# Decoder on one core: tags carried behind the scattered rows, and the last pair's routing in portions of 3 and 1 tiles

## What is computed

```python
xf = x.reshape(N, C)                                   # 2048 tokens, the cross attention's normalised result
topv, topi = jax.lax.top_k(xf @ Wr + br, 2)            # two of 8 experts a token
gates = jax.nn.softmax(topv, axis=-1)
sel = one_hot(topi, E).sum(1)
rank = jnp.cumsum(sel, axis=0) - sel                   # place of the token in its expert's list
keep = (sel > 0) & (rank < cap)                        # cap = 512 places an expert
buf[e, rank] = token                                   # tokens by expert and place
h = gelu(xpad[buf] @ W1 + b1); out = h @ W2 + b2
final[token] += out * gate                             # for each place of each expert
```

## Time and profile before

| | |
|---|---|
| runs | 2364.72, 2367.3, 2368.29 us; median 2367.3 |
| profiled execution | 2387.01 us |
| its span | 2384.8 us |
| PE busy | 2072.3 us, 87% of the span |
| DVE busy | 1717.6 us, 72% |
| ACT busy | 1045.8 us, 44% |
| POOL busy | 334.0 us, 14% |
| mean granted clock of PE | 0.933 |

### The profile page before, as it was taken

How to read it: one execution, slowest core, us unless ns; L and a number is a source line. 1 busy time by engine, 2 the same in 40 slices (tenths; PEclk the granted TensorE clock), 3 DMA queues, 4 the chain that set the end, 5 groups by cost and what they waited for, 6 DMA issues and landing times.

```text
span 2384.8 us, 33574 instructions
## 1 busy us (share of the span) xinstructions
PE 2072.3 (87%) x12364; PEld 1260.1 (53%) x12364; DVE 1717.6 (72%) x2514; ACT 1045.8 (44%) x1641; POOL 334.0 (14%) x368
## 2 busy tenths in 40 slices
PE   6999999999999999885768887988788889839998
PEld 4666666666666666551323344444354445516665
DVE  6677777777777778869999899989998995210001
ACT  1223333322322222237765867587758872202221
POOL 1111111111111111100000000000000001362222
PEclk8999999999999999997789987989899999969999
DMA  6000000000000100011110111011101113112442
GB/s 242 2 0 19 28 26 1 18 28 26 1 18 10 50 2 1 1 38 47 49 60 19 44 52 42 19 36 60 35 19 43 53 36 116 49 26 62 125 124 49
DMA packets 62238, 99.80 MB, mean 42 GB/s; under 512 B 13332, under 2 KB 44591, under 8 KB 61584
## 3 DMA queue, kind: packets, MB, share of 16 engines
q1 hardware_dynamic: 55120, 90.10, 11.6%
q0 software_dynamic: 6976, 7.84, 1.7%
HBM read 83.53 MB, written 15.53 MB: 42 GB/s over the span
## 4 chain that ended last, share of the span: by engine, by line
PE 53%; DVE 28%; issue 10%; ACT 4%; DMA 2%; another core or an unknown queue 1%; POOL 0%; DVEq 0%; SPq 0%; ACTq 0%; POOLq 0%
PE po L1810 9%; PE pa L1800 9%; DVE arena L1561 8%; PE pa L1758 4%; PE po L2378 4%; DVE arena L1551 4%; PE pt L1775 3%; PE pa L2084 3%; PE pa L2367 3%; DVE arena L1158 2%; DVE arena L1569 2%; DMA arena<-rows_to_experts 2%; PE pa L1790 1%; DVE arena L1160 1%; PE pt L1783 1%
## 5 line engine op out<-in xcount | busy, mean ns | idle before, releaser
L2084 PE MATMUL pa<-arena 128*128 128x512 f32 x512 | 297.9, 711 | 85.8 <-DVE arena L1569 85.8
L1561 DVE TENSOR_TENSOR_SCAN arena<-arena 128x1024 f32<-128x1024 f32 x128 | 292.5, 2285 | 13.5 <-ACT arena L937 13.3
L580 POOL TENSOR_SCALAR arena<-arena 128x2 f32<-128x2 f32 (+1 forms) x92 | 27.4, 298 | 1528.2 <-DVE arena L1426 824.7
L1810 PE MATMUL po<-arena 128*128 128x256 f32 x960 | 224.2, 385 | 0.0
L2084 PEld LDWEIGHTS pa<-arena 128*128 128x128 f32 x512 | 100.8, 216 | 218.8 <-DVE arena L1569 117.4
L1800 PE MATMUL pa<-arena 128*128 128x512 f32 x480 | 212.5, 595 | 4.4 <-ACT arena L754 4.1
L776 ACT COPY arena<-pa 128x512 f32<-128x512 f32 x128 | 65.7, 600 | 324.1 <-PE pa L1758 324.1
L1233 DVE TENSOR_TENSOR arena<-pa,arena 128x512 f32<-128x512 f32 x256 | 158.7, 682 | 63.1 <-PE pa L1758 63.0
L921 ACT ACTIVATE arena<-arena 128x510 f32<-128x510 f32 x256 | 170.7, 718 | 55.1 <-DVE arena L1561 51.8
L1810 PEld LDWEIGHTS po<-arena 128*128 128x128 f32 x960 | 176.8, 189 | 32.9 <-issue 6.0
L1701 DVE TENSOR_TENSOR arena<-po,arena 128x512 f32<-128x512 f32 x14 | 9.7, 692 | 231.2 <-PE po L2378 231.2
(11 more groups left out here) (268 smaller groups left out, 3706.6 us busy)
## 6 DMA issues: line engine op xcount, KB each, us to landing
arena<-bc_rows SPq DMA_DIRECT2D x64, 512.0 KB, 4.2
arena<-in_L_ffn_W SPq DMA_DIRECT2D x16, 1024.0 KB, 8.7
arena<-in_L_attn_W SPq DMA_DIRECT2D x8, 1024.0 KB, 5.5
rows_to_experts<-arena SPq DMA_DIRECT2D x4, 1024.0 KB, 13.0
arena<-rows_to_experts SPq DMA_DIRECT2D x8, 512.0 KB
out<-arena SPq DMA_DIRECT2D x5, 512.0 KB, 8.7
arena<-in_x SPq DMA_DIRECT2D x4, 512.0 KB, 7.0
arena<-in_rows SPq DMA_DIRECT2D x8, 256.0 KB, 3.2
```

Source lines behind the costliest of these rows:

```text
L1561: v.tensor_tensor_scan(h.rearrange(flat), decay.rearrange(flat), h.rearrange(flat), 0.0, ALU.mult, ALU.add).then_inc(scan_done, 1)
L1810: last = mm(po[s][:, ts(i, D)], gT[:, c, ts(tile, P)], w2[:, c, :], start=c == 0, stop=c == FM - 1)
L2084: last = mm(pa[c][:, :], ident, uh[i % len(uh)][:, n, :], start=g == 0 and n == 0, stop=g == NS // NG - 1 and n == NG - 1)
```

## The change

**Tags ride behind the rows.** The tile `hst` that holds the rows to be scattered becomes a view of a wider tile `tagged`, 260 numbers a row: the 256 features, then the token's number, its two gates, and the first place of its best expert. A row scatter sends all 260, so `rows_to_experts` has rows of 1040 bytes, and the 32 tag scatters, their DRAM buffer and the tag loads are gone. DVE copies the token numbers into the tile in `weighed`, and per expert finds in `slots_of` which of the two gates belongs to this expert (is the first place of the token's best expert that of this expert or not). The expert part of DVE's program is written out instead of looped, since this comparison needs the expert's number as a constant. `send_rows` now also waits for `tags_ready`.

**The fill.** The zeros go to the first 256 numbers of each row, runs of 1024 bytes instead of 8192; the filling tags go to the last four, 4096 runs of 16 bytes. ACT and POOL wait for both.

**Three portions.** The first 12 tiles are routed as before. The last pair's tiles 12 to 14 get bias, statistics and scaling while the last tile's attention is still under way, and are routed, placed and scattered (6 scatters) as a second portion; tile 15 follows as a third (2 scatters). PE, ACT, DVE and POOL get programs of their own for this. In the first portion, `send_rows` waits for at most 13 of the last pair's 16 value products where it waited for up to 16.

```diff
+TAG = 4
+LAST_TILE = NT - 1
+LAST_THREE = NT - TT
...
-    hst = keep(NT, D)
+    tagged_at = keep.at
+    tagged = keep(NT, D + TAG)
+    hst = tagged[:, :, 0:D]
...
-    lt, rk, base, over = ([a(NT) for _ in range(2)] for _ in range(4))
-    tags = [a(NT, 2) for _ in range(2)]
-    gate = [one[:, :, 1] for one in tags]
+    lt, rk, over = ([a(NT) for _ in range(2)] for _ in range(3))
+    tokens = a(NT)
+    token, gate, base = tagged[:, :, D], [tagged[:, :, D + 1 + k] for k in range(2)], [tagged[:, :, D + 3], a(NT)]
...
-    slot_tags, slot_rows = [a(TT, 2) for _ in range(2)], [a(TT).bitcast(I32) for _ in range(2)]
+    slot_rows = [a(TT).bitcast(I32) for _ in range(2)]
+    slot_gate, slot_part = [a(TT) for _ in range(2)], a(TT)
...
-    xg, xgT, gTe, ye = [a(TT, D) for _ in range(2)], a(KC, W), a(EF // P, W), [a(TT, D) for _ in range(2)]
+    xg, xgT, gTe, ye = [a(TT, D + TAG) for _ in range(2)], a(KC, W), a(EF // P, W), [a(TT, D) for _ in range(2)]
...
-    rows_to = nc.dram_tensor("rows_to_experts", (NE * CAP, D), F32, kind="Internal").ap()
+    rows_to = nc.dram_tensor("rows_to_experts", (NE * CAP, D + TAG), F32, kind="Internal").ap()
-    tags_to = nc.dram_tensor("tags_to_experts", (NE * CAP, 2), F32, kind="Internal").ap()
...
         for q in range(4):
-            sp.dma_start(rows_to.rearrange("(q p r) d -> q p (r d)", q=4, p=P)[q], zero).then_inc(zeroed, 16)
-        sp.dma_start(tags_to, t["tags"]).then_inc(tags_set, 16)
+            sp.dma_start(rows_to.rearrange("(q p r) d -> q p r d", q=4, p=P)[q][:, :, 0:D], zero.rearrange("p (r d) -> p r d", d=D)).then_inc(zeroed, 16)
+        sp.dma_start(rows_to[:, D:D + TAG], t["tags"]).then_inc(zeroed, 16)
...
-            sp.wait_ge(xr_ready, p + 1)
+            sp.wait_ge(xr_ready, p + 1 if p < PAIRS - 1 else PAIRS + 1)
         sp.wait_ge(scattered, 16 * 2 * NT)
         for j in range(2):
             expert_rows(j, j)
-        sp.wait_ge(tags_sent, 16 * 2 * NT)
-        for j in range(2):
-            slot_tags_in(j, j)
...
         def send_rows(first, end, places):
-            pool.wait_ge(zeroed, 16 * 4)
+            pool.wait_ge(zeroed, 16 * 5)
             pool.wait_ge(places_ready, places)
-            pool.wait_ge(xf_kept, end // TT + 1)
+            pool.wait_ge(tags_ready, places)
+            if places == 1:
+                pool.wait_ge(xf_kept, PAIRS)
+            else:
+                pool.wait_ge(xr_ready, PAIRS + places - 2)
             for i in range(first, end):
                 if places == 1:
-                    pool.wait_ge(av2_done, 16 * (PAIRS - 1) + i + 5)
+                    pool.wait_ge(av2_done, 16 * (PAIRS - 1) + min(i + 5, 13))
                 for k in range(2):
                     nc.gpsimd.indirect_dma_start(
-                        out=rows_to, out_offset=bass.IndirectOffsetOnAxis(ap=into[k][:, i:i + 1], axis=0), in_=hst[:, i, :], in_offset=None,
+                        out=rows_to, out_offset=bass.IndirectOffsetOnAxis(ap=into[k][:, i:i + 1], axis=0), in_=tagged[:, i, :], in_offset=None,
                         bounds_check=NE * CAP - 1, oob_is_err=False).then_inc(scattered, 16)
...
             if p is None and n is None:
-                send_rows(0, NT - TT, 1)
+                send_rows(0, LAST_THREE, 1)
+                deviations(GROUPS + groups + 1, 0, TT - 1)
+                deviations(GROUPS + groups + 2, TT - 1, 1)
+                send_rows(LAST_THREE, LAST_TILE, 2)
+                send_rows(LAST_TILE, NT, 3)
+                return
...
-        send_rows(NT - TT, NT, 2)
-        for i in range(NT):
-            for k in range(2):
-                nc.gpsimd.indirect_dma_start(
-                    out=tags_to, out_offset=bass.IndirectOffsetOnAxis(ap=into[k][:, i:i + 1], axis=0), in_=tags[k][:, i, :], in_offset=None,
-                    bounds_check=NE * CAP - 1, oob_is_err=False).then_inc(tags_sent, 16)
...
-                    act.wait_ge(zeroed, 16 * 4)
+                    act.wait_ge(zeroed, 16 * 5)
...
+            def last_rows_out(done, bank, tile, count):
+                act.wait_ge(last_turned, done)
+                nc.scalar.copy(xrT[:, :, tile * P:(tile + count) * P], bank.rearrange("p (k t) -> p k t", k=KC)).then_inc(last_copied, 1)
...
-                        top_gates(0, NT - TT, 1)
+                        top_gates(0, LAST_THREE, 1)
+                    if i == 35:
+                        last_rows_out(1, po[1][:, :], 0, 2)
+                        last_rows_out(2, pt[1][:, 0:S], 2, 1)
+                top_gates(LAST_THREE, LAST_TILE, 2)
+                last_rows_out(3, po[1][:, 0:S], 3, 1)
+                top_gates(LAST_TILE, NT, 3)
...
+            v.tensor_scalar(token[:, at], tokens[:, at], 0.0, None, ALU.add)
...
+            def last_statistics(first, end):
+                rows = xst[:, q * TT + first:q * TT + end, :]
+                dve.wait_ge(wo2_out, 4 * q + end)
+                step.after(v.tensor_tensor(rows, rows, wide(r_xo, end - first), ALU.add))
+                for i in range(first, end):
+                    last = v.bn_stats(out=stats[:, i, :], in_=xst[:, q * TT + i, :])
+                step.apart(last)
+                for i in range(first, end):
+                    last = v.bn_aggr(out=mv[:, i, :], in_=stats[:, i, :])
+                last.then_inc(var_ready, 1)
+            def last_scaled(k, first, end):
+                dve.wait_ge(rstd_ready, cross_group + k)
+                for i in range(first, end):
+                    last = v.tensor_scalar(xr[:, i, :], xst[:, q * TT + i, :], mv[:, i, 0:1], rstd[:, i:i + 1], ALU.subtract, ALU.mult)
+                last.then_inc(xr_ready, 1)
...
+                    if i == 30:
+                        last_statistics(0, TT - 1)
+                    if i == 31:
+                        last_scaled(1, 0, TT - 1)
...
+            if at.lone:
+                last_logits(q + 1, pt[1], LAST_THREE, LAST_TILE)
+                dve.wait_ge(logits_ready, q + 1)
+                compared(LAST_THREE, LAST_TILE)
+                counted(LAST_THREE, LAST_TILE)
+                chosen(LAST_THREE, LAST_TILE)
+                cross(UNITS + 3 + drain)
+                last_statistics(TT - 1, TT)
+                weighed(LAST_THREE, LAST_TILE, 2)
+                ranked(LAST_THREE, LAST_TILE, 2)
+                placed(LAST_THREE, LAST_TILE)
+                last_scaled(2, TT - 1, TT)
+                last_logits(q + 2, pt[0], LAST_TILE, NT)
+                dve.wait_ge(logits_ready, q + 2)
+                compared(LAST_TILE, NT)
+                counted(LAST_TILE, NT)
+                chosen(LAST_TILE, NT)
+                weighed(LAST_TILE, NT, 3)
+                ranked(LAST_TILE, NT, 3)
+                placed(LAST_TILE, NT)
+                return
...
+        def slots_of(e):
+            j = e % 2
+            dve.wait_ge(xg_in[j], 16 * (e // 2) + 16)
+            first, second, best = xg[j][:, :, D + 1], xg[j][:, :, D + 2], xg[j][:, :, D + 3]
+            v.tensor_scalar(slot_rows[j], xg[j][:, :, D], 0.0, None, ALU.add).then_inc(slot_rows_ready, 1)
+            v.scalar_tensor_tensor(slot_part, best, float(CAP * e), first, ALU.is_equal, ALU.mult)
+            step.after(v.scalar_tensor_tensor(slot_gate[j], best, float(CAP * e), second, ALU.not_equal, ALU.mult))
+            step.after(v.tensor_tensor(slot_gate[j], slot_gate[j], slot_part, ALU.add))
...
+        def expert_out(e):
+            j, q = e % 2, e // 2
+            dve.wait_ge(we_in[j], 64 * q + 64)
+            if q:
+                dve.wait_ge(ye_added[j], 16 * TT * q)
+            slots_of(e)
+            for s in range(2):
+                dve.wait_ge(down3_done[j], 2 * q + s + 1)
+                v.tensor_tensor(two(ye[j], s), po[s][:, :].rearrange("p (t d) -> p t d", t=2),
+                                b2e[j].unsqueeze(1).broadcast_to([P, 2, D]), ALU.add).then_inc(down3_out[j], 1)
+                dve.wait_ge(down3_out[j], 2 * q + s + 1)
+                for i in (2 * s, 2 * s + 1):
+                    v.tensor_scalar(ye[j][:, i, :], ye[j][:, i, :], slot_gate[j][:, i:i + 1], None, ALU.mult).then_inc(ye_ready[j], 1)
+        for e in range(NE - 1):
+            expert_out(e)
+        last_expert_out(NE - 1)
...
+            def last_rows(bank, tile, count):
+                for c in range(KC):
+                    for i in range(count):
+                        last = transposed(bank[:, ts(count * c + i, P)], xr[:, tile + i, ts(c, P)])
+                last.then_inc(last_turned, 1)
+            def last_router(copied, bank, first, end):
+                pe.wait_ge(last_copied, copied)
+                for i in range(first, end):
+                    for c in range(KC):
+                        last = mm(bank[:, ts(i - first, NE)], xrT[:, c, ts(i, P)], w_r[:, c, :], start=c == 0, stop=c == KC - 1)
+                last.then_inc(route_done, 1)
...
             if at.lone:
                 pe.wait_ge(at2_ready, 4 * q + TT - 1)
```

(23 more changed lines are left out.)

116 lines of the change are left out of this document (34 added, 82 removed).

## The result

| | before, beside it | changed |
|---|---|---|
| runs, us | 2364.72, 2367.3, 2368.29, 2369.21, 2369.42 | 2349.58, 2354.4, 2354.58, 2357.0, 2363.64 |
| median | 2368.29 | 2354.58 |
| ratio, 95% interval | | 0.9942, 0.9922 to 0.9962 |
| profiled execution, its span | 2387.01, 2384.8 | 2349.58, 2347.8 |
| PE; POOL busy | 2072.3; 334.0 | 2063.1; 303.4 |

The time lies in the predicted range of 2352 to 2371 and the sign is right, though it is 0.4 us under the 2355 to 2365 that I forecast most. The gain is nearly twice the forecast's 7.4; by the interval of the ratio it is 9 to 18 us.

The account below looks back on a forecast made before the run. It took timed runs to be bound by the tags at about 2153 us, without ACT's gaps. Gains 5.2, 2.0, 0.5 and 0.7 make 8.4, less 1.0 is 7.4: 2360 plus or minus 5, range 2352 to 2371.

Parts of the forecast that it names:

- What bounds the kernel: Around expert 0: timed runs lack the profile's gaps and are bound by the tags at about 2153 us.
- the gaps: Three waits of 10.45, 10.44 and 7.64 us between ACT's first gelus of expert 0, in the first profile of before.
- rival B: ACT's gaps in expert 0 are in timed runs too; the full 28.6 us comes off, to 2339; chance 0.08.
- Row load 5.2 earlier: Three portions leave two scatters after the last places; SP loads the experts' rows at 2103.5 instead of 2108.67.
- Rival E: Last tile's places come 5 us later than thought, through DVE or a slow PE; time 2365; chance 0.07.
- Load of the rows 2.0 shorter: Experts' first row load takes 6.5 us instead of 8.48, as no tag scatters run beside it.
- lower bound of 4.9: Shortest row load allowed: same bytes at 75 ns, 32 packets an engine, plus 2.13 us landing and some issue.
- The 6.5: Time in us taken for the experts' row load, between bounds of 4.9 and 9.5.
- Gate and tags, 1.2 together: End of expert 0: 0.5 us from fewer gate steps, 0.7 us since PE and not the tags ends it.
- Later loads plus 1.0: Row loads of experts 2, 4 and 6 cost 0.3 us more each for 1040-byte packets; bounds 0 and 3.
- rival C: Rows' loads become slower, as 1040-byte rows start off 256-byte boundaries; time 2364 to 2366; chance 0.15.
- rival D: Start of program: 4096 small fill writes make ACT wait in the first pair; 2377 at 150 ns each; chance 0.10.

Follow-up runs that it names:

- portions_only: The kernel before with only the three routing portions added, tag scatters and tag loads kept; median 2362.04 us, ratio to before 0.9961 to 0.9987.
- after_tags: The changed kernel with the 32 small tag scatters put back right behind the last row scatter, read by nobody; median 2358.10 us.
- again: The kernel before, unchanged, profiled in a second execution; 2370.07 us.
- tags_only: The kernel before with only the tagged rows and their use in the experts, routing still in two portions; median 2360.86 us, ratio 0.9956 to 0.9984.
- tags_later: The changed kernel with the 32 small tag scatters put back, but held until both experts' first rows have landed; median 2356.02 us.
- after_1024: The changed kernel with rows of 256 numbers on 1024-byte boundaries, the fill of before, and tags loaded once from a constant block; median 2352.61 us.

## Why the prediction was right, and where its sizes were off

- **What bounds the kernel: right.** That the gaps are not in the timed runs, on which the whole size hung, was tested with one more execution and held, and the timed medians fit it; rival B falls.
- **Row load 5.2 earlier: right.** Measured 5.5 by the cut profiles (131.3 less 125.8), 5.2 by portions_only alone. The steps came out 0.9 to 1.7 us early throughout: row minimum 2066.1 (2067), last value product 2073.8 (2074.9), logits 2079.1 (2080.1), choice 2083.3 (2084.4), places 2088.2 (2089.5), row load 2102.2 (2103.5). Of that 1.0 was there from the token load on and is scatter between executions. Rival E falls. What was not asked is whether the order that costs 3.2 us at the row minimum was needed.
- **Load of the rows 2.0 shorter: the term that was mis-sized.** It is 3.9 to 4.9 shorter (7.58 and 8.53 to 3.66), and 3.66 us lies under my lower bound of 4.9. I kept the 75 ns a packet of a stretch in which the scatters ran as the floor of that bound; without them a packet takes 51 ns. The row had the disturbance in it that the change removes, so it could bound nothing from below. The packets' mean is also the smaller part: 33 packets an engine at 51 instead of 75 ns save 0.8 us, and the sum that gives 4.9 would have given 4.9 for the kernel before too, where the load took 8.48. What the sum lacked was the slow start that the windows of after_tags show. The 6.5 itself was a middle value with no row behind it.
- **Gate and tags, 1.2 together: right.** From the end of the second eviction to SP's weight load 2.17 us in again (2152.84 to 2155.01), 0.68 in the changed kernel: 1.5.
- **Later loads plus 1.0: wrong sign.** The piece behind expert 0 is 2.9 to 5.4 us shorter. About 1.3 of it (9.78 to 8.46) lies behind the last scatter. The rest is expert 2's rows: they took 11.21, 11.84 and 11.65 us in the three profiles of kernels with tag loads, whose own tag load is issued right behind them, and 9.6 and 9.7 in tags_only and the changed kernel, where they land before expert 1's up products end; and SP issued them 1.5 us nearer to PE's work. In after_tags and tags_later, with tag scatters but no tag loads, they took 10.0 and 10.2, so it is likely the tag load that costs, though no run took it out alone. PE's stall of 1.4 us to 3.04 us there, and the lower clock behind the longest one, went away. I had charged the change for longer packets and not credited it with what runs beside them.
- **Alignment (rival C): nothing**, by after_1024; the 40 beats that the prediction works out are the worst place of a row, not the mean.
- **Fill at the start (rival D): hidden.** Issued at 26.2 it lands 15.5 us later, at 41.7, in my 38 to 55, and ACT, which waits for it, goes on at 58.23 when PE is ready:

```profile
53.87 2.05 ACT L771 COPY arena<-pa 128x512 f32<-128x512 f32 x4 [13.40 <-PE pa L1791]
58.23 0.58 ACT L734 COPY arena<-po 128x512 f32<-128x512 f32 x1 [2.31 <-PE po L1770]
```

  The 4096 writes of 16 bytes cost the time nothing visible, whatever the read-modify-write below 512 B takes that the Trainium skill names (DMA: Bandwidth & Descriptors, Specifications).
- **Sum.** 5.5 + 3.9 + 1.5 + 0.4 (up products, 16.05 to 15.70) + 2.9 is 14.2, against 13.7 measured. The first and the last term are against the first profile, the middle three against again; with again throughout the sum is 19, so that it meets 13.7 this closely is partly luck. Two terms were off in the same direction, the load by 1.9 to 2.9 us and the piece behind expert 0 by 4 to 6, and put the time just outside 2360 plus or minus 5; the stated range held it because its lower end had been set 3 us below that. The text also said that a time below 2350 would mean B; one run fell there (2349.58, the profiled one) without gaps, so the mark was set too near.
